# Relative-position attention on one core: score tiles in groups of four, the values after the relative block, six exponentiated tiles

## What is computed

```python
def proj(W, b):
    return (hidden_states @ W.T + b).reshape(B, L, NUM_HEADS, HEAD).transpose(0, 2, 1, 3)
q, k, v = ...
attn = jnp.einsum('bhld,bhrd->bhlr', q, k) * scale
dist = jnp.arange(L)[None, :] - jnp.arange(L)[:, None]
dist = jnp.clip(dist, -LEFT, RIGHT) + LEFT        # LEFT, RIGHT = 64, 8
rel = jnp.einsum('bhld,lrd->bhlr', q, dist_emb[dist]) * scale
attn = jax.nn.softmax(attn + rel, axis=-1)
out = jnp.einsum('bhlr,bhrd->bhld', attn, v)
out = out.transpose(0, 2, 1, 3).reshape(B, L, H)
return out @ Wo.T + bo
```

## Time and profile before

| | us |
|---|---|
| median of 3 runs | 1584.43 |
| lowest, highest | 1580.87, 1585.0 |
| the profiled execution: its own time, first to last instruction (its span) | 1594.0 |
| mean granted TensorE clock in it | 0.917 of full speed |

### The profile page before, as it was taken

How to read it: one execution, slowest core, us unless ns; L and a number is a source line. 1 busy time by engine, 2 the same in 40 slices (tenths; PEclk the granted TensorE clock), 3 DMA queues, 4 the chain that set the end, 5 groups by cost and what they waited for, 6 DMA issues and landing times.

```text
span 1594.0 us, 31010 instructions
## 1 busy us (share of the span) xinstructions
PE 1381.8 (87%) x10918; PEld 958.7 (60%) x10918; DVE 1023.3 (64%) x2477; ACT 725.5 (46%) x1467; POOL 541.6 (34%) x548
## 2 busy tenths in 40 slices
PE   4999999999999789723379878999999998969998
PEld 2566666666666456511267545666766666647887
DVE  3576766667666677478123338687887877857554
ACT  2566666666666355300023234454555554524222
POOL 1455555555555200000711355533433433211110
PEclk7899999999999899655789779999999999979999
DMA  3323101011010200000022123211211211000000
GB/s 131 106 85 109 35 23 35 23 35 35 23 35 24 60 1 2 0 1 0 16 71 86 40 54 109 43 48 29 45 45 27 50 39 29 21 1 1 1 0 26
DMA packets 91921, 61.40 MB, mean 39 GB/s; under 512 B 26841, under 2 KB 78890, under 8 KB 91830
## 3 DMA queue, kind: packets, MB, share of 16 engines
q1 hardware_dynamic: 89206, 58.68, 13.3%
q0 software_dynamic: 2048, 1.27, 0.3%
q10 hardware_dynamic: 576, 0.20, 0.0%
HBM read 21.63 MB, written 10.49 MB: 20 GB/s over the span
## 4 chain that ended last, share of the span: by engine, by line
PE 74%; DVE 16%; ACT 3%; issue 3%; another core or an unknown queue 2%; DMA 1%; ACTq 0%; SPq 0%; POOL 0%; DVEq 0%
PE psum L1070 8%; PE psum L1083 8%; PE psum L1060 7%; PE psum L1445 7%; PE psum L1558 5%; PE psum L1436 5%; PE psum L1457 4%; PE psum L1569 4%; PE psum L1430 3%; DVE negmax L2105 2%; PE psum L1037 2%; PE psum L1278 2%; PE psum L1046 2%; PE psum L1090 2%
## 5 line engine op out<-in xcount | busy, mean ns | idle before, releaser
L581 POOL TENSOR_TENSOR arena<-arena,rden 128x512 f32<-128x512 f32 x256 | 261.1, 1041 | 252.9 <-DVE rden L1669 252.9
L763 ACT ACTIVATE arena<-psum,negmax 128x512 f32<-128x512 f32 x256 | 173.8, 683 | 135.9 <-DVE negmax L1660 134.9
L2105 DVE TENSOR_REDUCE negmax<-psum 128x1 f32<-128x512 f32 x256 | 165.1, 685 | 63.1 <-PE psum L1436 53.5
L1660 DVE TENSOR_REDUCE negmax<-psum 128x1 f32<-128x512 f32 x256 | 164.3, 684 | 11.1 <-PE psum L1060 7.7
L1070 PE MATMUL psum<-cst,arena 128*128 128x128 f32 x1024 | 144.0, 280 | 1.4 <-DVE w L1655 0.4
L1070 PEld LDWEIGHTS psum<-cst,arena 128*128 128x128 f32 x1024 | 108.8, 141 | 53.0 <-issue 50.8
L1060 PE MATMUL psum<-a_qk 64*128 64x512 f32 x768 | 124.9, 430 | 0.0
L1436 PE MATMUL psum<-w,wqkv 128*64 128x208 f32 x1024 | 123.0, 362 | 0.0
L641 POOL TENSOR_TENSOR a_qblk<-a_qstack,cst 96x512 fp32r<-96x512 f32 x64 | 68.8, 1074 | 146.2 <-PE psum L1436 136.9
L939 ACT ACTIVATE kT<-psum,negmax 128x512 f32<-128x512 f32 x64 | 44.0, 688 | 139.4 <-PE psum L1445 78.1
L1430 PE MATMUL psum<-a_kstack,a_qblk 96*128 96x512 f32 x256 | 98.3, 466 | 8.6 <-POOL wqkv L644 8.6
(11 more groups left out here) (319 smaller groups left out, 2811.4 us busy)
## 6 DMA issues: line engine op xcount, KB each, us to landing
hst<-hT SPq DMA_DIRECT2D x32, 256.0 KB, 2.3
a_kstack<-a_khi SPq DMA_DIRECT2D x128, 64.0 KB
wst<-wqkv SPq DMA_DIRECT2D x32, 192.0 KB, 2.4
w<-in_ew SPq DMA_DIRECT2D x2, 2048.0 KB, 8.7
a_kstack<-a_klo SPq DMA_DIRECT2D x64, 64.0 KB
xs_rows<-f SPq DMA_DIRECT2D x3, 1024.0 KB, 5.6
arena<-xs_rows SPq DMA_DIRECT2D x8, 384.0 KB, 3.7
ys_rows<-wqkv SPq DMA_DIRECT2D x8, 384.0 KB, 2.7
```

The source lines that it names most:

```text
L581: pool.tensor_tensor(a0_p[u % 4], a0_p[u % 4], rden[:, u:u + 1].broadcast_to([P, SEQ]), ALU.mult).then_inc(a0_norm, 1)
L763: act.activation(a0_p[u % 4], bank[u % 4][:, :], ACT.Exp, bias=negmax[:, u:u + 1], accum_out=den[:, u:u + 1]).then_inc(a0_exp, 1)
L1660: dve.tensor_reduce(negmax[:, u:u + 1], bank[u % 4][:, :], AX.X, ALU.max, negate=True).then_inc(a0_max, 1)
L2105: dve.tensor_reduce(negmax[:, n % 8:n % 8 + 1], bank[n % 4][:, :], AX.X, ALU.max, negate=True).then_inc(a1_max, 1)
```

## The change

- TensorE runs a turn as four **quads** of four tiles: four L1430, each with its own wait for the exponential of four tiles back, then sixteen L1436 records. At quads 1 and 3 the values come next, ahead of the transposes. Then two transposed tiles of the quad before, the features (quad 2), the guests of both p of the quad, the other two transposed tiles, and back or project last.
- ScalarE: exp, exp, copy, exp, exp, copy; the guests of both p after that.
- VectorE: max, max, (values copy), copy, (add), max, max, (features), copy, then key ends (quad 0), normalise, statistics, and the guests of both p.
- `ptile` has six tiles, two of them over constants of the first layer (`C_CQ`, `C_SQ`), and exp waits for the transposes of six tiles back.
- `x1_norm` of the third batch, which runs in the turns of the fourth, stands one slot p earlier (7 becomes 6).
- Semaphores, DMAs, GpSimd's program and the arithmetic stay as they are.

The diff; of the turns' old code, which is printed above, the removed lines are left out:

```diff
-        ptile = [hst[:, :], qT[:, :], kT[:, :], vtok[:, :, :].rearrange("p a b -> p (a b)")]
+        ptile = [hst[:, :], qT[:, :], kT[:, :], vtok[:, :, :].rearrange("p a b -> p (a b)"),
+                 cst[:, C_CQ:C_CQ + SEQ], cst[:, C_SQ:C_SQ + SEQ]]
+        PT = len(ptile)
...
@@ ScalarE
-                if it or n >= 4:
-                    act.wait_ge(a1_t, it * 16 + n - 3)
-                act.activation(ptile[n % 4], bank[n % 4][:, :], ACT.Exp, bias=negmax[:, n % 8:n % 8 + 1]).then_inc(a1_exp, 1)
+                if it * 16 + n >= PT:
+                    act.wait_ge(a1_t, it * 16 + n - PT + 1)
+                act.activation(ptile[(it * 16 + n) % PT], bank[n % 4][:, :], ACT.Exp, bias=negmax[:, n % 8:n % 8 + 1]).then_inc(a1_exp, 1)
             def a1_turn(it):
+                for quad in range(4):
+                    a1_exp_of(it, 4 * quad)
+                    a1_exp_of(it, 4 * quad + 1)
+                    if quad:
+                        a1_copy(it, 4 * quad - 3)
+                    elif it:
+                        a1_copy(it - 1, 13)
+                    if quad == 1 and it < NT - 1:
                         high_k(it + 1)
+                    a1_exp_of(it, 4 * quad + 2)
+                    a1_exp_of(it, 4 * quad + 3)
+                    if quad:
+                        a1_copy(it, 4 * quad - 1)
                     elif it:
+                        a1_copy(it - 1, 15)
+                    for p in (2 * quad, 2 * quad + 1):
...
@@ TensorE
+            def a1_scores(it, quad):
+                hg, j, t = quad // 2, quad % 2, it % QT
+                if quad == 0:
                     pe.wait_ge(a1_kin[it % 2], (it // 2 + 1) * STACK)
+                pe.wait_ge(a1_qb, it * 8 + quad * 2 + 2)
                 first_key = window(t)
+                for n in range(4 * quad, 4 * quad + 4):
                     lg = n % 4 * 2
+                    if it or quad:
+                        pe.wait_ge(a1_exp, it * 16 + n - 3)
+                    pe.matmul(bank[n % 4][:, :], qblk[:, hg, j, lg:lg + 2, :, :].rearrange("p g h l -> p (g h l)"), kstack[it % 2][:, quad, :],
                               start=True, stop=False)
+                for n in range(4 * quad, 4 * quad + 4):
                     for blk in range(2):
...
+            def a1_guest(it, p):
+                free = {0: 2 * it - 1, 3: 2 * it, 4: 2 * it, 7: 2 * it + 1}.get(p)
+                for of, part, done in ((pre_of, pre_part, pre_done), (x1_of, x1_part, x1_done), (f1_of, f1_part, f1_done)):
+                    if of(it, p):
+                        pe.wait_ge(*guest[0])
+                        pe.wait_ge(a1_oc, free)
+                        part(*of(it, p))
+                        guest[0] = done(*of(it, p))
+
             def a1_turn(it):
+                for quad in range(4):
+                    a1_scores(it, quad)
+                    if quad == 1 and it:
+                        pe.wait_ge(*guest[0])
+                        a1_values(it - 1, 1)
+                    if quad == 3:
                         pe.wait_ge(*guest[0])
                         a1_values(it, 0)
+                    before, last = (it, 4 * quad - 4) if quad else (it - 1, 12)
+                    if it or quad:
+                        a1_turn_t(before, last)
+                        a1_turn_t(before, last + 1)
+                    if quad == 2 and it:
+                        a1_feats(it - 1)
+                    a1_guest(it, 2 * quad)
+                    a1_guest(it, 2 * quad + 1)
+                    if it or quad:
+                        a1_turn_t(before, last + 2)
+                        a1_turn_t(before, last + 3)
+                    if quad == 1 and it:
+                        a1_back(it - 1, 1)
+                    if quad == 2 and it:
+                        a1_project(it - 1)
+                    if quad == 3:
+                        a1_back(it, 0)
...
@@ VectorE (a1_guest holds the guest steps as they stood, with 6 for 7)
             def a1_turn(it):
+                for quad in range(4):
+                    a1_maximum(it, 4 * quad)
+                    a1_maximum(it, 4 * quad + 1)
+                    if quad == 1 and it:
+                        a1_out(it - 1, 1)
+                    if quad == 3:
+                        a1_out(it, 0)
+                    if quad:
+                        a1_copy(it, 4 * quad - 4)
                     elif it:
+                        a1_copy(it - 1, 12)
+                    if quad == 3 and it:
+                        a1_add(it - 1)
+                    a1_maximum(it, 4 * quad + 2)
+                    a1_maximum(it, 4 * quad + 3)
+                    if quad == 2 and it:
+                        a1_feats(it - 1)
+                    if quad:
+                        a1_copy(it, 4 * quad - 2)
+                    elif it:
+                        a1_copy(it - 1, 14)
+                    if quad == 0 and it < NT - 1:
                         key_ends(it + 1)
+                    if quad == 1 and it:
+                        a1_normalise(it - 1, 1)
+                    if quad == 3:
+                        if it:
                             a1_stats(it - 1)
                         a1_normalise(it, 0)
+                    a1_guest(it, 2 * quad)
+                    a1_guest(it, 2 * quad + 1)
```

More of the change, by code:

```diff
@@ L1444, in a1_turn_t @@
                 for kt in range(QT):
-                    mm = pe.transpose(bank[4 + n % 2][:, kt * P:(kt + 1) * P], ptile[n % 4][:, kt * P:(kt + 1) * P], ident)
+                    mm = pe.transpose(bank[4 + n % 2][:, kt * P:(kt + 1) * P], ptile[(it * 16 + n) % PT][:, kt * P:(kt + 1) * P], ident)
                 mm.then_inc(a1_t, 1)
@@ L1490, in _ @@
             guest = [(pa_vc, 1)]
-            def a1_turn(it):
[L1493 to L1511, removed]
+            def a1_guest(it, p):
[6 more added lines that the diff above has]
+                        guest[0] = done(*of(it, p))
@@ L2133, in a1_stats, with a1_guest @@
                 norm_stats(it)
[L2135 to L2155 removed]
+            def a1_guest(it, p):
+                b, s = it // QT, it % QT * 8
+                for step in pre_steps(it, p):
+                    pre_norm((it + 1) // QT + 1, step)
+                if pre_of(it, p):
+                    pre_part(*pre_of(it, p))
+                at = s + p - (8 if b < B - 1 else 6)
+                if b and 0 <= at < 6:
+                    x1_norm(b - 1, at)
+                if x1_of(it, p):
+                    x1_part(*x1_of(it, p))
+                for step in f1_steps(it, p)[1]:
+                    f1_norm(f1_steps(it, p)[0], step)
+                if f1_of(it, p) and f1_of(it, p)[1] == 1:
+                    f1_scores(f1_of(it, p)[0])
@@ L2156, in a1_turn @@
                             a1_stats(it - 1)
-                    if p == 6:
-                        a1_out(it, 0)
-                    if p == 7:
                         a1_normalise(it, 0)
-                    for step in pre_steps(it, p):
-                        pre_norm((it + 1) // QT + 1, step)
-                    if pre_of(it, p):
-                        pre_part(*pre_of(it, p))
-                    at = s + p - (8 if b < B - 1 else 7)
-                    if b and 0 <= at < 6:
-                        x1_norm(b - 1, at)
@@ L2168, in a1_turn @@
-                    if x1_of(it, p):
-                        x1_part(*x1_of(it, p))
-                    for step in f1_steps(it, p)[1]:
-                        f1_norm(f1_steps(it, p)[0], step)
-                    if f1_of(it, p) and f1_of(it, p)[1] == 1:
-                        f1_scores(f1_of(it, p)[0])
+                    a1_guest(it, 2 * quad)
+                    a1_guest(it, 2 * quad + 1)
             for it in range(NT):
```

63 lines of the change are left out of this document (6 added, 57 removed).

## The result

The changed kernel takes 1598.9 us in the median of 7 runs (1590.2 to 1602.1), the kernel before 1582.9 (1580.7 to 1585.0): ratio **1.0087, 95% interval 1.006 to 1.0114**. By the ratio it is slower by 14 us (16 between the two medians) where 15 us less were forecast. The time lies inside the stated range (1547 to 1602), on the wrong side.

What follows compares the result with a forecast made beforehand. It took the stage to be bound by TensorE, VectorE close behind. 16 x 25.9 + 13 + 32 = 459, say 460, against 475.7 us: -15 from 1584.4, so 1569 us; range 1547 to 1602 (the forecast's own 1557 to 1579).

Steps and rivals of the forecast that it cites:

- The seams: TensorE's switches between 128 and 64 output columns, 0.33 us each: fewer save 1.7 us a turn, 28 us in sixteen.
- The loop of a group: Bare schedule: 5.35 us without values, 7.22 with, 6.15 in the third group; a turn 25.9 us against 24.3.
- Guests get it back: TensorE guests up to 1.0 us hide in spare time; projections stick out by 13 us, VectorE's guests by 32.
- waits, clock dips and the first turns: Some 49 us of the old stage beyond sixteen bare turns (389 us) and about 38 us of TensorE guests.
- evacuation becomes the bound, slower than before: Rival: guests do not use the spare time, so loop and guests add; +9 to +25 us, 1596 us, chance 0.23.
- guests of TensorE delaying the copies: In the slower rival: the wait for a free guest bank ahead of the values may delay a group's first copy.
- point of decision: The slower rival decides once less than about 25 us of the 38 us of TensorE guests is hidden.
- Six tiles: Six exponentiated tiles instead of four: cost 0, no added instruction, and no stall removed that could be named.
- the term 0: GpSimd's staging, DMA and key stack keep their order, with some 5 us of slack a turn: cost 0.
- A mean of a row: VectorE's Newton round priced at about 1.2 us: three instructions of some 0.4, two at 0.45 and 0.41.

Runs made afterwards that it cites:

- u_early_only: Changed kernel with norm steps of even slots in groups 1 and 3 alone moved ahead of VectorE's copies: 0.9956 of the kernel before.
- the fillers: Twelve idle transposes in groups 2 and 3 of turns 3, 7, 10, 11, added to the changed kernel (1.0033) and to q_again's kernel (0.9881, 0.9889).
- q_again: Repeat: changed kernel, values between transpose halves, features behind third maximum, even-slot norm steps of groups 1 and 3 before first copy: 0.9892 of the kernel before.
- r_again: Repeat: q_again's kernel plus twelve idle transposes in groups 2 and 3 of turns 3, 7, 10 and 11: 0.9889 of the kernel before.
- p_filler: Changed kernel plus twelve idle transposes between transpose halves in groups 2 and 3 of turns 3, 7, 10, 11: 1.0033 of the kernel before.

## Why the prediction was wrong

**The seams: right.** Sixteen L1436 take 1.63 us, twice 0.92 less 0.21. (1.7 us in each of sixteen turns are 27, not 28; the forecast doesn't use the product.) **The loop of a group: right**, 5.35 us of 5.35, 7.1 to 7.4 of 7.22, 6.33 to 6.5 of 6.15, a bare turn 26.0 of 25.9. So the bare order loses 1.7 us a turn, 25 us in fifteen, as it said.

**"Guests get it back": this step failed.** The forecast had the changed stage at the bare turns + 13 + 32 us: 13 for projections of TensorE that stick out, 32 for norm steps of VectorE. Over fifteen turns the profile has 456.4 - 15 x 26.0 = 66 us beside the bare turns (84 before: 448.7 - 15 x 24.3). Without norm steps it has 421.4 - 390 = 31 (before 417.7 - 364.5 = 53). So VectorE's norm steps cost 35 us; 32 was well sized. What was missed is the rest, 31 where 13 stood. Of the 49 us of "waits, clock dips and the first turns" of the kernel before, the norm steps are 31; the other 18 were simply dropped from the sum of the new order, a term put at nothing without a reason, as if spare time in a group took them up. They stayed: turns 2 and 3 alone, without any norm steps, are 36.4 and 34.2 us, 19 of the 31 above the bare turns (34.6 and 30.4, 16 above, in the old order), with a projection beside GpSimd's gathers and staging, VectorE's key ends behind them (5.38 us) and the clock down. 390 + 13 + 35 + 18 = 456. The forecast mixed sixteen turns with what is counted here in fifteen, so 18 is good to some 3 us; and the causes inside it (GpSimd, clock, projections) weren't taken apart by a run.

**Why nothing took them up.** The spare time is real in a bare group, but it stands in one place, behind a copy on VectorE. When VectorE is late by a guest, the wait for its first copy grows by the same time, and two steps in a row are late together, where a pair order let a maximum pass between them. `u_early_only` shows this for turn 7; that it is the same in every turn is argued. The rival "evacuation becomes the bound, slower than before", with 1596 us and a chance of 0.23, is what happened in size and in place: guests weren't hidden enough. Its picture of guests of TensorE delaying the copies wasn't; VectorE's guests do, and through a guest's bank also the values (turn 3). Its point of decision, less than 25 of 38 us hidden, is met by this count: beside the norm steps 53 us became 31. That 1596 lies 3 us from the measured time is in part luck, since its own sum left the clock and the waits as open as the forecast did. The Trainium skill, TensorEngine Tiling (Array Packing), PSUM Bottleneck, says that tiling speeds up TensorE but not the copies out of PSUM, which may then become the bottleneck. The trace fits that as far as it goes: the seams went, and the wait left in the bare group is the one for a copy out of PSUM (0.44 us). Both kernels use the array in the same shapes, so no run here tests the rule.

**Six tiles: mis-sized.** "It costs no instruction ... removes no stall" priced them against the old order; in the new one they are worth 2.1%. The schedule of 5.35 us assumed them, so this didn't move the forecast.

**GpSimd: the term 0 was right for its own queue and wrong for VectorE's.** A mean of a row (L1988 at 0.41) hid instructions of 0.16 and of 0.92 us, and in other lines single ones took 4 to 5. The Trainium skill, SBUF — State Buffer, section Who interferes with whom, says that a VectorE instruction with two SBUF inputs contends with a GpSimd instruction that reads SBUF and that the loser is blocked for the whole of the other. The traces agree, and go further: the expert sum in turn 3 waited through four of GpSimd's in a row, while maxima and copies out of PSUM kept 0.69 beside GpSimd (two maxima in 1.27 at 1153.18).

**Open.** The profiles have 8 us of the medians' 14 in the stage; the rest isn't placed, since the profiled execution of before was itself 10 us slow. How much of the loss is TensorE's clock and how much the stalls under it, the fillers didn't settle; 46 us at the lower level for 27 are 19 more at half the rate, which bounds the clock's share at some 10 us (an estimate). Whether norm steps placed where GpSimd is idle, or `f1_norm` placed as the others were, would help further wasn't tried.

## What to carry to other kernels

Spare time of an engine counts only where it stands: ask which queue ends it, and whether what you mean to hide there delays that same queue. A regrouping that makes the bare schedule longer by 7% in trade for slack should place the irregular work by hand first: here the place of twelve small steps decided 16 us of the stage, twice what the regrouping lost there. With them and the rearranged values the order of four tiles is faster than the kernel before, by 1.1 to 1.4% in its two comparisons and by 9 us (0.6%) in the stage, so how much faster is known only roughly. And keep, in the sum of the new order, every wait of the old one for which you can't name what removes it.

## What the runs showed of the hardware

Two things were not expected. A VectorE instruction with both inputs in SBUF was held up through several successive GpSimd instructions (4.39 us for work of 0.34, 5.38 for work of 0.68). And twelve idle transposes in a stall of 2 to 3 us lengthened nothing that the intervals can tell, while the granted clock of the stage rose from 0.95 to 0.98 (`q_again` to `r_again`; to 0.96 in `p_filler`).
